# Half of each feed-forward issued with its own section's front, the gated half multiplied in place

## What is computed

```python
xn = _layernorm(x, axis=-1)
# attention: token-shift mixes, low-rank projections, r, w, k, v, g, kk, a, then
S = S * dt[:, :, None, :] + sa[..., None] * bt[:, :, None, :] + vt[..., None] * kt[:, :, None, :]
y = jnp.einsum('bhij,bhj->bhi', S, rt)
# group norm of y, bonus, gate, output projection -> s
# feed-forward, 256 -> 768 -> 256, integer weights times 1/127:
h = jax.nn.silu(gate) * up
g = _silu(_L0_ffn_ref(xn, w_gate, w_up, w_down))
x = x + s * g
```

## Time and profile before

| | us |
|---|---|
| median of 3 runs (1609.95 to 1610.18) | 1610.09 |
| span of the profiled execution | 1603.4 |
| its PE busy | 1520.5 |
| its DVE busy | 1243.6 |
| its ACT busy | 1069.5 |
| its POOL busy | 354.6 |

### The profile page before, as it was taken

One profiled execution on the slowest core, in us unless ns is written; L12 is line 12 of the kernel. 1 busy time (PEld: TensorE's weight loads), 2 busy tenths in 40 slices (PEclk: granted clock), 3 DMA queues, 4 the chain that ended last, 5 costly groups with the idle time before them and its releaser, 6 DMA issues.

```text
span 1603.4 us, 48245 instructions
## 1 busy us (share of the span) xinstructions
PE 1520.5 (95%) x20288; PEld 1064.9 (66%) x20288; DVE 1243.6 (78%) x2661; ACT 1069.5 (67%) x1889; POOL 354.6 (22%) x362
## 2 busy tenths in 40 slices
PE   3699999999999999999999999999999999999887
PEld 1366767576676757667676676757667675766765
DVE  2968787787878878887887878778787887888643
ACT  3758586685857758685775858668585775768512
POOL 3121402313040131302213140231304013130201
PEclk9799999999999999999999999999999999999999
DMA  4011110301212021111202111030121202111020
GB/s 149 14 25 29 33 34 16 62 18 32 43 25 47 16 55 25 33 34 24 56 16 39 42 34 34 16 62 19 33 42 25 48 16 55 25 33 34 12 56 28
DMA packets 251430, 57.85 MB, mean 36 GB/s; under 512 B 223696, under 2 KB 250704, under 8 KB 251088
## 3 DMA queue, kind: packets, MB, share of 16 engines
q1 hardware_dynamic: 241936, 41.95, 13.9%
q10 hardware_dynamic: 9280, 12.81, 2.2%
HBM read 36.38 MB, written 18.35 MB: 34 GB/s over the span
## 4 chain that ended last, share of the span: by engine, by line
PE 92%; DVE 3%; ACT 2%; issue 1%; POOL 0%; DMA 0%; SPq 0%; ACTq 0%; DVEq 0%; POOLq 0%
PE bank L534 23%; PE chunk L380 15%; PE bank L544 11%; PE bank L509 8%; PE bank L664 4%; PE chunk L642 3%; PE chunk L614 3%; PE chunk L589 3%; PE chunk L598 2%; PE bank L485 2%; PE bank L380 2%; PE bank L517 2%; PE bank L479 2%; PE chunk L628 2%; DVE VU L981 1%
## 5 line engine op out<-in xcount | busy, mean ns | idle before, releaser
L1325 POOL TENSOR_TENSOR SF<-ST,CT 128x256 f32<-128x256 f32 x128 | 99.7, 779 | 728.8 <-DVE ST L1211 728.8
L534 PE MATMUL bank<-xT,wg 128*128 128x256 f32 x768 | 197.2, 391 | 14.2 <-DVE VU L981 13.5
L534 PE MATMUL bank<-xT,wu 128*128 128x256 f32 x768 | 207.3, 395 | 0.0
L544 PE MATMUL bank<-wd,hT 128*128 128x256 f32 x768 | 176.8, 383 | 1.9 <-DVE hT L1171 1.9
L534 PEld LDWEIGHTS bank<-xT,wg 128*128 128x128 f32 x768 | 136.3, 189 | 57.6 <-DVE VU L981 24.1
L544 PEld LDWEIGHTS bank<-wd,hT 128*128 128x128 f32 x768 | 143.3, 190 | 29.3 <-issue 7.2
L534 PEld LDWEIGHTS bank<-xT,wu 128*128 128x128 f32 x768 | 135.1, 188 | 34.8 <-issue 14.5
L380 PE MATMUL chunk<-KS,W 128*128 128x512 f32 x320 | 149.6, 598 | 0.3 <-ACT gT L719 0.3
L509 PE MATMUL bank<-qpad,KS 128*64 128x32 f32 x4096 | 141.2, 226 | 4.0 <-DVE KE L1143 4.0
L887 ACT ACTIVATE Y<-chunk 32x256 f32<-32x256 f32 x256 | 96.3, 376 | 70.9 <-PE chunk L598 67.0
L509 PEld LDWEIGHTS bank<-qpad,KS 128*64 128x64 f32 x4096 | 130.7, 141 | 14.1 <-issue 9.0
(11 more groups left out here) (156 smaller groups left out, 3231.3 us busy)
## 6 DMA issues: line engine op xcount, KB each, us to landing
smalls<-in_x SPq DMA_DIRECT2D x32, 256.0 KB, 3.1
Y<-in_x SPq DMA_DIRECT2D x32, 256.0 KB, 3.0
out<-fsil ACTq DMA_DIRECT2D x32, 256.0 KB, 2.6
scrA<-AM SPq DMA_DIRECT2D x64, 64.0 KB, 1.9
hat<-scrB SPq DMA_DIRECT2D x32, 128.0 KB, 3.1
hat<-scrF SPq DMA_DIRECT2D x32, 128.0 KB, 3.1
KE<-scrA SPq DMA_DIRECT2D x64, 32.0 KB, 2.2
scrT<-KE SPq DMA_DIRECT2D x16, 128.0 KB, 1.7
```

The lines of the kernel that those rows point to most:

```text
L534: q = pe.matmul(o[:, TT_ * n2:TT_ * n2 + TT_], w[:, h, 128 * (n + n2):128 * (n + n2) + 128], x_now[:, h], start=(h == 0), stop=(h == NH - 1))
L544: q = pe.matmul(o[:, 256 * m:256 * m + 256], hT[:, n, 128 * m:128 * m + 128], wd[:, n, :], start=(n == 0), stop=(n == NF - 1))
L1325: pool.tensor_tensor(SF[:, :, :, :], ST[:, :, :, :], fade[:, c].unsqueeze(3).to_broadcast([128, B, NH, N]), ALU.mult).then_inc(*faded.up)
```

## The change

The feed-forward is now issued one half earlier. A stream N in a round consists of what is left of the feed-forward of section i - 1 and then the first half (b = 0) of the feed-forward of section i (`feed`, `LEAD`). The first section round so gets the conversion and the first half of feed-forward 0; the round of the last front has an order of its own (`CLOSE`), and the last back has only the second half of feed-forward 15 beside it. The buffer `sg` is gone: ACT writes the silu of the gate into `hT`, and DVE multiplies it there. `fsil` becomes three half buffers, used in turn. All order strings are new; the diff shows only the code.

```diff
-        sg = sb("sg", [128, COLS])
-        fsil = sb("fsil", [128, NM, C])
+        fsils = [sb(f"fsil{i}", [128, NM // 2, C]) for i in range(3)]
...
+        def fsil_of(t, b):
+            return fsils[(2 * t + b) % 3]
...
         def run(engine, norm, mixing, decays, key, receptance, value, update, pairs, ffn, back, output, convert):
+            begun = {}
+
+            def feed(last, first):
+                if last is None:
+                    yield from convert()
+                else:
+                    yield from begun.pop(last)
+                if first is not None:
+                    begun[first] = ffn(first)
+                    yield from itertools.islice(begun[first], LEAD[engine])
+
             for tn, tf, tb, to in sections():
-                streams, order = {}, LAST if tn is None and tf is None else FIRST if tb is None and to is None else ORDER
+                streams = {}
+                order = LAST if tn is None and tf is None else FIRST if tb is None else CLOSE if tn is None else ORDER
...
+                if tf is not None or tb is not None:
+                    streams["N"] = feed(tb, tf)
                 if tb is not None:
-                    streams["N"], streams["B"] = ffn(tb), back(tb)
-                elif tf is not None:
-                    streams["N"] = convert()
+                    streams["B"] = back(tb)
...
+LEAD = {"pe": 14, "act": 4, "dve": 3, "pool": 0}
...
             def ffn(t):
-                u = 0
...
-                        if u or t:
-                            act.wait_ge(*h_made(t, u))
-                        act.activation(sg[:, :], ring.tile(key)[:, :], ACT.Silu).then_inc(*sg_ready.up)
-                        u += 1
+                        if n == 0 and (b or t):
+                            act.wait_ge(*ring.full((t, "down", b - 1) if b else (t - 1, "down", B - 1)))
+                        act.activation(hT[:, n:n + 2, :], ring.tile(key)[:, :].rearrange("p (n c) -> p n c", n=2), ACT.Silu).then_inc(*sg_ready.up)
...
-                    if t:
-                        act.wait_ge(*stored(t - 1))
+                    if 2 * t + b >= 3:
+                        act.wait_ge(*stored((2 * t + b - 3) // 2))
...
-                        if b and n == 0:
-                            dve.wait_ge(*ring.full((t, "down", b - 1)))
-                        i = dve.tensor_tensor(hT[:, n:n + 2, :], sg[:, :].rearrange("p (n c) -> p n c", n=2),
+                        i = dve.tensor_tensor(hT[:, n:n + 2, :], hT[:, n:n + 2, :],
```

More of the change, by code:

```diff
@@ L1 @@
+import itertools
 from contextlib import ExitStack
@@ L51 @@
 CTOT = _at
[L53 to L61, removed]
+ORDER = {"pe": ("NNNFKNOOFNNNKNNVOONKRKVNRNBKBRNNBBNBBNBVNBNVBBNNBBEBVBBNBBNBVBBNNBBXBXBBNBBNBXBBXBBXBXBBNBBLBNBBXXBB"
+                "XLXXXLL"),
+         "act": ("FNKFFFFFFKNNKVKKEKRBVBKXRROKXBOXBDNVNBVVBBVBNBBXBBVVBBBBNXBBBXXBBBLLLXBXNBBBBLXX"),
+         "dve": ("OBNOOBBBBBDBBBBBBDBDBBDNOBBOXKKEFDNEKDDDKEXKEBXXBEXNBXBXXXBXBEXXEXBXXXXBNXXBLBXXXBXXXBNLXBXXXXBLXLBB"
+                 "XXXXBXLLLLLLLL"),
+         "pool": ("BDBBBBBLBBLBLLLLLLLL")}
+FIRST = {"pe": ("FKFKKVKVKVRRRVEVVXXXXXXLNXXXNLXXLLNNNNNNNNNNXNN"),
+         "act": ("FKFFFFFFKKVKKKEKKRRVRXXDVVXVVVXXVXXLXLLXNLXNNXN"),
+         "dve": ("NDDNNDDKKEFKKDXEEDXKDEDEXXXEXXXXXXXXXXEXXXLXXLXXXXXXXXXXXLXXLXXXLLLLLLLLNNN"),
          "pool": ("DLLLLLLLLLL")}
-LAST = {"pe": ("NOOONONNNNNNNNNBBNNNBBBBBNBBBBBNBBBBBNBBBBBNBBBNBBNBBBBBNBBBBBNBBBNBBNNNNN"),
-        "act": ("NONNOBBNBBBBBBBBNBBBBBBBBBNBBBBBBBBNN"),
-        "dve": ("BOOOBBBBBBBBBBBBBBBBONONNBBBBBBBBBBBNBBBBBNBN"),
+LAST = {"pe": ("NOOONONNBBNNNNBBBBBNBBBBBNBBBBBNBBBBBNBBBBBBBBBBBBBBBBBBBBNN"),
+        "act": ("NBBBNBBBBBBBBBBBBBBBBBBBBBBNOBBON"),
+        "dve": ("BOOBBBBOBBBBBBBBBBBBONOBBBBBBBNBBBBBBBBBNB"),
         "pool": ("BBBBBBBBB")}
+CLOSE = {"pe": ("NNFKOONNFNNNKROONNNVKVKRNRNBKBNNNBBBVBBNBNBNBEVBBNBBVBBBBBNBNBBBBBNBBBXXBBNBBXVBNXXBBXNBBBXBBNBXXBXX"
+                "XNN"),
+         "act": ("FNKFFFFFFNRNKVKKVKEKBRRBKOXKDOBXBNVVBBNBXVBVBBBBBNBBBVXXBBBXXBNVBXBBBBXBXBXN"),
+         "dve": ("OOOBNBBBDBBBBBFODBBNBDDBOBBBBXDDKKDEENDXKKEKEBXXBEXXBXNEBXXXBBEXXBXXBBBNXXXXBBXXXXXXXXXBXBXXBXXBXXXN"
+                 "XB"),
+         "pool": ("BDBBBBBBBB")}
+LEAD = {"pe": 14, "act": 4, "dve": 3, "pool": 0}
 NB = 4
@@ L865, in ffn @@
                     act.wait_ge(*ring.full(key))
-                    if t:
-                        act.wait_ge(*stored(t - 1))
-                    act.activation(fsil[:, 2 * b:2 * b + 2, :], ring.tile(key)[:, :].rearrange("p (m c) -> p m c", m=2), ACT.Silu).then_inc(*fs_ready.up)
+                    if 2 * t + b >= 3:
+                        act.wait_ge(*stored((2 * t + b - 3) // 2))
+                    act.activation(fsil_of(t, b)[:, :, :], ring.tile(key)[:, :].rearrange("p (m c) -> p m c", m=2), ACT.Silu).then_inc(*fs_ready.up)
                     yield f"ffn{b}"
@@ L922, in output @@
                     act.wait_ge(*o_ready(t, m2 + 1))
-                    act.dma_start(rows(x_out, t, m2), fsil[:, 2 * m2:2 * m2 + 2, :]).then_inc(*stored.up)
+                    act.dma_start(rows(x_out, t, m2), fsil_of(t, m2)[:, :, :]).then_inc(*stored.up)
                     yield f"out{m2}"
@@ L1243, in output @@
                     dve.wait_ge(*ring.full(key))
-                    fs, xo = fsil[:, 2 * m2:2 * m2 + 2, :], ym[:, 2 * m2:2 * m2 + 2, :]
+                    fs, xo = fsil_of(t, m2)[:, :, :], ym[:, 2 * m2:2 * m2 + 2, :]
                     dve.wait_ge(*fs_ready(t, m2 + 1))
```

## The result

The changed kernel takes 1632.95 us in the median of four runs (1631.27 to 1633.60), the kernel before 1610.02 (1609.24 to 1610.18). That is 22.9 us more. The ratio of the runs is 1.0149, 95% interval 1.0134 to 1.0165 (the quotient of these two medians, 1.0142, lies inside it). The span of the profiled execution is 1629.8 us, 26.4 more than before; that difference is larger than the one of the medians because the profiled execution of the kernel before was a short one.

What follows compares the result with a forecast made beforehand. PE was taken to bound the middle, chains the two ends. 14.2 - 2.0 - 2.6 - 2.7 - 1.9 - 2.4 - 1.2 + 0.5 = +1.9 us: span 1605.3, run 1612.0 us, range 1602 to 1619.

Steps and rivals of the forecast that it cites:

- First and second round: Start to the second section's masks: first round +14.2 us for the added half feed-forward, second -2.0 for fewer waits.
- Thirteen middle rounds: Middle sections: fewer changes between wide and narrow products, 55 to 53 a round, -0.2 us each; -2.6 us in all.
- a new wait in every middle round: Rival, middle rounds: the band comes late by 0.5 us in each of 13, giving 1618 us; chance 0.14.
- The product in place and the buffers: Silu written into hT and multiplied there, half buffers: no new wait that costs time, 0 us.
- Closing round: Up to section 14's last output: a down product and changes of kind leave, states without filler add; -2.7 us.
- To the first values: From section 14's last output to the last recurrence's first values: 36.3 us against 38.2, -1.9 us.
- Recurrence: Last recurrence: nine half-tile fillers become four, 0.5 us saved for each of five, rounded down to -2.4 us.
- The rival of the half clock: Last recurrence at half clock: at most 1.4 us a chunk, 11 us, giving 1623, or 1617 if halved; chance 0.10.
- Tail: Behind the recurrence: the last down product starts some 2 us earlier and is off the way; -1.2 us.
- Clock: Before the last band PE idles about 6 us, so band, corner and eight half tiles run slow; +0.5 us.
- A run is 6.7 us above the span: Whole kernel: run time taken as the profiled span plus 6.7 us, so span 1605.3 gives 1612.0 us.

Runs made afterwards that it cites:

- inplace_only: Kernel before, with only the silu of the gate written into hT and multiplied in place, no sg: 1608.98 us, ratio 0.9999.
- close_old: Changed kernel with the middle strings of the kernel before, in middle and closing rounds; first and last strings stay changed: 1617.80 us, ratio 1.0058.
- last_filled: first_gap with another last string: four half tiles before the band, one after chunk 1's first two products, one behind each of chunks 1 to 7: 1626.34 us.
- before_swap: Kernel before, with one half tile and the key tile ahead of the transposes exchanged in PE's middle string: 1606.55 us, ratio 0.9988.
- before_best: before_swap with the first string of the changed kernel: 1604.46 us, ratio 0.9985.
- first_gap: close_old with four half tiles moved ahead in the first round and DVE's second bonus product earlier: 1616.29 us, ratio 1.0048.
- before_best2: The same code as before_best, compared once more with the kernel before: 1603.47 us, ratio 0.9961.
- last_warm: first_gap with no half tile before the band, five between corner and chunk 1, one behind each of chunks 1 to 7: 1618.18 us, ratio 1.0064.
- last_spread: close_old with the last recurrence's four half tiles behind chunks 1, 3, 5 and 6 instead of 1 to 4: 1623.59 us, ratio 1.0083.

## Why the prediction was wrong, point by point

- **First and second round, +12.2 forecast, +11.9 measured.** The mechanism was right: first keys at 70.78 (forecast near 70.7), first tile of the second round at 108.97 (forecast 109.6). That the places agree to 0.6 us is luck in part. The ten profiled executions with this first string and the changed phase had their first keys between 70.53 and 76.42. What repeats is the distance from the keys to that tile, 38.2 us where the forecast has 38.9, and 20.7 to 21.7 with the old string.

```profile
70.78 3.63 PE L530 MATMUL bank<-qpad,KS 128*64 128x32 f32 x64 [1.46 <-DVE KE L1162]
...
108.97 1.89 PE L555 MATMUL bank<-xT,wg 128*128 128x256 f32 x8
```

- **Thirteen middle rounds, -2.6 forecast, +13.9 measured.** This step failed, and with it the sign. It counted changes between wide and narrow products and left the 1.36 us of waiting as it was, "Bounds: -1.5 a round if it goes too, +0.5 if a new wait comes". The term was wrong in both parts: the count gave no gain (PE was busy 0.29 us longer in a section), and the waiting did not stay, since three new waits came and one went. The rival "a new wait in every middle round" was right in kind, but named the band as its place and 0.5 us as its size; it was the bank chain behind the transposes (0.57), the new state (0.33) and Y (0.15). What it needed stood in the trace of the kernel before: the chain of 9.3 us, to be set against the PE work that the new order leaves beside it.
- **The product in place and the buffers, 0.** Right: inplace_only, 0.9999.
- **Closing round, -2.7 forecast, +2.1 measured.** The mechanisms were named (states without a filler), their sizes were wrong. PE's busy time fell by 2.1 us (87.19 to 85.07), where the terms of the sum that are work make 4.4; its idle time grew by 4.2 (1.94 to 6.12), where those that are waits make 1.7. close_old shows that it is the string and not the phase.
- **To the first values, -1.9 forecast, -1.1 measured.** The forecast is 36.3 us from the end of L619's product at 1541.07, measured were 37.1. The last table was asked for on time, at 1574.64, 33.6 us behind it. The first values followed 3.5 us later and not 2.8, because four half tiles at half clock (1572.06 to 1578.13) stood in front of them; in last_filled, with no tile there, it was 2.7 (1562.64 to 1565.37).
- **Recurrence, -2.4 forecast, -0.3 measured.** One chunk did shrink from 3.69 to 3.14; the next took 4.11 at the low clock, and the last ones stayed at it. The rival of the half clock, 0.10, was right from the second unfilled chunk on. Its price, at most 1.4 us a chunk, fits an unfilled chunk (4.11 less 3.14) and is too low for a filled one (5.49 less 3.69, 1.8). Its 11 us came in full with the kernel before's own last string (before_swap, before_best: 10.8 us). What the prediction set against it, that the first round kept its clock at about that busy share, did not hold here.
- **Tail, -1.2 forecast, 0 measured.** The down product was still in the way, since it ran 8.44 us at half clock and not 5.45.
- **Clock.** Forecast +0.5. The gap before the last band was 3.25 us and not about 6, and the band ran at full clock (1.15 us, as before); the corner and the four half tiles behind it were slow. The rest of the price belonged to the terms above. The Trainium skill, "TensorE: Matmul & The Clock Gate", section "HAM oscillation", says that work in bursts starts each burst cold. last_filled agrees: behind 5.24 us of waiting its recurrence began at the low clock. The changed kernel's recurrence and before_swap's are another case: there the clock fell with no wait of PE above 0.54 us in the chunk before.
- **A run is 6.7 us above the span.** Wrong. The changed kernel's profiled execution took 1631.27 for a span of 1629.8, 1.5 more. The kernel before's own was one of its short ones; its executions ran from 1604 to 1616 us. So the 6.7 us were mostly the difference between a short execution and the median.

So of the 26.4 us: 11.9 at the start go with the phase and this first string. Of them 10.7 lie between the first and second masks, where first_gap pays 8.5; the other 1.2 are less than the scatter of the first masks. 13.9 in the middle and 2.1 in the closing round are the strings. The end gives back 1.4 us in the changed kernel; in any variant, and with the closing round, at best 1.9 against the kernel before's profiled execution and 1.0 against before_best2's. It is bound by the inversion, its DMAs and the recurrence, and without the half tiles the clock fell there each time.

## What to carry to other kernels

Work taken from a stretch that a chain bounds gives little back (here 1.4 us of 15.6), and where the clock falls without it, its absence is paid: here 0.55 us was saved on one chunk, and the next then took 0.97 more than that one. When an order of instructions changes, list for each bank the chain that empties it and sum the PE work that stands beside it in the new order; here a wait removed at one tile came back at the next until that sum was larger than the chain. Judge such edits by the length of one section in the trace, which repeats to 0.1 us in all but a few sections of a run, and not by a median whose ends scatter by 10.

## What the hardware showed that was not expected

- A recurrence of narrow products, PE 84% busy, kept the granted clock at 1.00 with a 1.1 us wide product behind every chunk (last_warm, 28 us), and lost it within two chunks without one (changed kernel and nine variants with its last string; last_spread). The wide products are no warrant: before_swap and before_best have one behind every chunk and lost the clock in the first chunk, for most of the next 30 us. At the low clock a filled chunk took 5.49 us, an unfilled one 4.11.
- The same strings at the end gave 179.8 us (kernel before) and 191.0 us (before_swap) from the last masks on, with the granted clock at 1.00 in the recurrence of the one and at 0.50 in most of the other's.
- A wait of 0.6 us stayed at its bank or went to the next one in three kernels and left the section at 96.2 us; 1.7 us of work ahead of both banks took 0.85 us off.
